# Gated cross-attention on one core: keys and values of all batches projected in the first six iterations of the second phase

## The chip, the cores and the metric

The kernel runs on one core of a Trainium2 chip. The metric is the device time of one execution in microseconds; the median of the runs is compared. TensorE (PE) multiplies matrices, VectorE (DVE), ScalarE (ACT) and GpSimd (POOL) work on tiles in SBUF, the first two also in PSUM, and SyncE (SP) issues DMAs.

## What is computed

`x` and `ctx` are 32 batches of 256 tokens with 256 features. A first layer attends from `x` to `ctx` by a symmetric divergence and adds an MLP, gated by `g_xattn`; then comes a linear layer on rounded (fp8) inputs. The second layer is what the change touches:

```python
# per batch; 16 heads of 16 features; x has gone through the first layer
xh  = layernorm(x)
q   = xh  @ w_q + b_q
k   = ctx @ w_k + b_k          # needs only the input ctx
v   = ctx @ w_v + b_v          # needs only the input ctx
att = softmax(mask(q k^T))     # 256 x 256 for each head
x   = x + gate * ((att v) @ w_o + b_o)
x   = x + gate * (silu(layernorm(x) @ fc1 + fc1_bias) @ fc2 + fc2_bias)
```

In this run nothing is masked.

## The kernel before

`phase_a` computes the first layer for all batches and leaves `X` (all 32 batches) in SBUF. `phase_b` is a software pipeline over the batches: in one iteration each engine works on eight batches at once, each at another stage. The letters are `n` (quantise, lag 0), `f` (fp8 linear, lag 1), `q` (queries, keys, values, lag 2), `m` (maxima of the scores, lag 3), `a` (exponentials and weighted values, lag 4), `o` (output projection, lag 5), `h` (MLP, first half, lag 6) and `w` (MLP, second half, and result, lag 7). With 32 batches there are 39 iterations. Those at the start and the end are written out, with the steps left out that have no batch yet or no more; the middle is a loop (`pipeline`, L51). Iteration 0 begins at 611.4 us of the profiled execution, iteration 6 at 731.6 us.

The order of the work on each engine is written out by hand, as the list of calls at the end of each engine's `iteration`. All waits are semaphore counts: `done(b)` is the count after batch `b`, `landed(b)` that of DMAs, whose semaphores alternate by parity.

Keys and values stand in it so. SyncE loads the transposed context of `f` (`load_context`, L1250). GpSimd splits it into a high and a low bf16 part (`context_parts`, L1373 and L1375). TensorE projects keys (`keys`, 12 matmuls) and, as the last step of the iteration, values (`values_in`, 12 matmuls); both are L1835. ScalarE writes the high part of the keys (L1498), VectorE the low part (`keys_low`, L1691), ScalarE copies the values to `V` (L1520), whose other 16 columns per head hold ones and give the sums of the softmax. SyncE spills keys to DRAM (`spill_keys`, L1262) and reads them back in another layout (`stack_keys`, L1279). Keys of an even and of an odd batch have one DRAM buffer each.

The score matrices of two heads at a time go twice through PSUM: `scores(i)` (L1875) for the row maxima (`maxima(i)`, VectorE, L1653), i from 0 to 7, and, one iteration later, `scores_transposed(i)` (L1892) for the exponentials (`exponential(i)`, ScalarE, L1471). Each kind has one PSUM tile, so `scores(i+1)` waits for `maxima(i)` and `scores_transposed(i+1)` for `exponential(i)`. The maxima go through two DMA transposes and two small DMAs into row 48 of `Q4` (`transpose_maxima`, `row_of_maxima`); `scores_transposed(0)` waits for them. Below, sc1 is `scores(1)` and scT7 is `scores_transposed(7)`.

Other steps on the path are: `attention_normalised` (VectorE, xh, L1742), which waits for rs2 from `inverse_std_2` on GpSimd (L1380, L1382); `mlp_normalised` (hn, L1634); `scaled` (v, L1716); `normalised_low` (xT, L1620) and `mlp_low` (hT, L1675), the low bf16 parts; `queries_low` (L1684), which waits for ScalarE's `queries_high` (L1490); `attended(t)` (L1698, L1703) and `attended_low` (L1709); `mlp_columns` (L1640); and on GpSimd `silu_parts` (L1401, L1404) and `output_bias` (L1423), which waits for xh. Four more PSUM banks are shared in turns by the other products (`TURNS`); a product waits for the last reader of the bank's previous tile.

VectorE's order before begins: hn, v, attended(0), maxima(0), xT low, attended(1), maxima(1), hT low, maxima(2), queries low, attended low, maxima(3), columns, and so on to maxima(4), keys low, attention update, maxima(5).

## Time and profile before

| | us |
|---|---|
| median of 3 runs | 1620.32 |
| lowest and highest | 1616.96, 1621.4 |
| span of the profiled execution, first to last instruction | 1614.4 |

| engine | busy us | share of the span | instructions |
|---|---|---|---|
| PE | 1486.5 | 92% | 14155 |
| DVE | 1316.4 | 82% | 3187 |
| ACT | 1135.2 | 70% | 2057 |
| POOL | 1034.7 | 64% | 1392 |

The profile shows one execution. A row of the timeline gives the start in us, the duration in us, engine, line, operation, the tile written and those read, the shape, how many instructions are merged in the row (x12), and in brackets the idle time before it with what ended it. Matmuls overlap, so that twelve of them take 1.47 us as a row and begin 1.31 us after one another as groups. A row of the windows gives the busy time of each engine in a stretch, TensorE's granted clock as a share of full speed, and the share of the DMA engines.

### The profile page before, as it was taken

What the parts mean: (1) busy time and instruction counts of PE and PEld (TensorE: products, weight loads), DVE (VectorE), ACT (ScalarE), POOL (GpSimd) and SP (SyncE); (2) the same over time, 40 slices, a digit from 0 to 9 for tenths busy, and PEclk for the clock granted to TensorE, in tenths of its full rate; (3) what the DMA queues carried; (4) which work ended last, traced back from release to release, by engine and by line L of the source; (5) the groups of instructions that cost most, each with busy time, mean ns of one, the idle gap of its engine ahead of it and who ended that gap; (6) DMA issues with size and microseconds to landing.
All of it is one profiled execution on the core that took longest, in us unless ns stands there. A gap on an engine that the chain in (4) does not pass through costs nothing.

```text
span 1614.4 us, 42641 instructions
## 1 busy us (share of the span) xinstructions
PE 1486.5 (92%) x14155; PEld 1144.6 (71%) x14155; DVE 1316.4 (82%) x3187; ACT 1135.2 (70%) x2057; POOL 1034.7 (64%) x1392
## 2 busy tenths in 40 slices
PE   4999999999999972668999999999999999999997
PEld 2788888888888861435667676777777776777666
DVE  4698888888888875778988889898988889898742
ACT  7798888888888742355666666666666666676664
POOL 4588888888888744224556565665656566565445
PEclk9999999999999995588999999999999999999999
DMA  7322222322222002332223232232223232232200
GB/s 228 96 80 66 91 72 65 96 66 69 93 65 71 2 1 92 80 119 73 80 80 87 73 85 80 85 87 81 83 78 92 72 91 74 86 85 84 64 16 22
DMA packets 197690, 125.45 MB, mean 78 GB/s; under 512 B 44400, under 2 KB 196848, under 8 KB 197360
## 3 DMA queue, kind: packets, MB, share of 16 engines
q1 hardware_dynamic: 197616, 124.48, 26.2%
q8 instruction: 44, 0.72, 0.2%
q14 instruction: 30, 0.25, 0.1%
HBM read 92.69 MB, written 25.17 MB: 73 GB/s over the span
## 4 chain that ended last, share of the span: by engine, by line
PE 48%; SPq 4%; DVE 3%; issue 2%; DMA 2%; POOL 2%; ACT 1%; POOLq 0%
PE b_bank L1835 28%; PE b_bank L1910 7%; PE b_scoreT L1892 4%; PE b_score L1875 4%; PE b_bank L1843 2%; PE b_bank L1987 1%; SPq L1306 1%; DMA b_nmT<-b_nm 1%; DMA b_yT<-b_y 1%; SPq L1290 1%; DVE b_nm L1653 1%; SPq L1279 1%; PE b_bank L1925 1%; ACT b_E L1471 1%; SPq L1315 0%
## 5 line engine op out<-in xcount | busy, mean ns | idle before, releaser
L1471 ACT ACTIVATE b_E<-b_scoreT 128x1024 f32<-128x1024 f32 x256 | 262.2, 1024 | 152.5 <-PE b_scoreT L1892 151.3
L1653 DVE TENSOR_REDUCE b_nm<-b_score 128x4 bf16<-128x1024 f32 x256 | 313.3, 1224 | 54.6 <-PE b_score L1875 48.4
L31 ACT ACT_TABLE_LOAD x157 | 201.4, 1283 | 18.6 <-PEq L1059 15.2
L1835 PE MATMUL b_bank<-f,b_YT 128*128 128x256 bf16 x1536 | 190.3, 274 | 4.7 <-POOL b_YT L1404 4.6
L890 PE MATMUL bank<-hT,W1T 128*128 128x256 bf16 x1536 | 183.3, 273 | 2.4 <-DVE hT L706 1.7
L1835 PE MATMUL b_bank<-b_hT,f 128*128 128x256 bf16 x1536 | 183.4, 273 | 0.8 <-DVE X L1749 0.8
L890 PE MATMUL bank<-W2T,G 128*128 128x256 bf16 x1024 | 171.0, 272 | 6.7 <-DVE GT L780 6.2
L1835 PEld LDWEIGHTS b_bank<-f,b_YT 128*128 128x128 bf16 x1536 | 143.5, 98 | 39.7 <-issue 19.5
L1835 PEld LDWEIGHTS b_bank<-b_hT,f 128*128 128x128 bf16 x1536 | 147.7, 98 | 30.3 <-issue 12.6
L890 PEld LDWEIGHTS bank<-hT,W1T 128*128 128x128 bf16 x1536 | 148.0, 98 | 27.7 <-ACT G L549 4.0
L1388 POOL TENSOR_TENSOR b_v<-b_v,b_e 128x512 f32<-128x512 f32 x32 | 40.6, 1269 | 195.0 <-DVE b_e L1734 195.0
L1404 POOL TENSOR_TENSOR b_YT<-b_Y,b_YT 128x512 bf16<-128x512 f32 x128 | 148.9, 1163 | 10.7
L1401 POOL TENSOR_SCALAR b_YT<-b_Y 128x512 bf16<-128x512 f32 x128 | 82.2, 642 | 104.2 <-ACT b_Y L1531 97.5
L1531 ACT ACTIVATE b_Y<-b_bank,b1f 128x256 f32<-128x256 f32 x256 | 104.2, 473 | 51.4 <-PE b_bank L1835 51.0
L890 PE MATMUL bank<-W2T,GT 128*128 128x256 bf16 x512 | 139.5, 273 | 0.0
L1910 PE MATMUL b_bank<-b_E,b_V 128*32 128x256 f32 x2048 | 134.0, 392 | 0.0
L1875 PE MATMUL b_score<-b_K,b_Q 48*128 48x256 bf16 x1024 | 102.7, 280 | 24.1 <-DVE b_nm L1653 13.1
L549 ACT ACTIVATE G<-bank,b1c 128x256 f32<-128x256 f32 x256 | 103.7, 467 | 29.4 <-PE bank L890 29.4
L890 PEld LDWEIGHTS bank<-W2T,G 128*128 128x128 bf16 x1024 | 98.3, 98 | 23.2 <-issue 12.6
L1892 PE MATMUL b_scoreT<-b_Q,b_K 49*128 49x256 bf16 x1024 | 100.7, 275 | 8.6 <-ACT b_E L1471 6.2
L1742 DVE TENSOR_SCALAR b_xh<-X,b_mv,b_rs 128x256 f32 (+1 forms) x64 | 61.9, 1006 | 43.7 <-POOL b_rs L1382 43.7
L1910 PEld LDWEIGHTS b_bank<-b_E,b_V 128*32 128x32 f32 x2048 | 57.7, 111 | 49.8 <-issue 23.4
(222 smaller groups left out, 3524.8 us busy)
## 6 DMA issues: line engine op xcount, KB each, us to landing
b_Q<-q_dram SPq DMA_DIRECT2D x192, 64.0 KB, 2.6
b_K<-k_dram SPq DMA_DIRECT2D x192, 64.0 KB, 2.8
xin<-in_x SPq DMA_DIRECT2D x32, 256.0 KB, 3.2
ctxn<-in_ctx SPq DMA_DIRECT2D x32, 256.0 KB, 2.8
mask_in<-in_mask SPq DMA_DIRECT2D x32, 256.0 KB, 3.0
X<-in_x SPq DMA_DIRECT2D x32, 256.0 KB, 4.0
ctxt<-in_ctxT SPq DMA_DIRECT2D x32, 256.0 KB, 4.2
b_ctxt<-in_ctxT SPq DMA_DIRECT2D x32, 256.0 KB, 2.8
```

The source lines that it names most:

```text
L31: act.add_instruction(mybir.InstLoadActFuncSet(name=nc.get_next_instruction_name(), act_func_set_id=which, ins=[], outs=[]))
L549: last = nc.scalar.activation(G[:, 2 * j + i], mlp_ps[j % 2][:, i], ACT.Gelu, bias=b1c[:, 2 * j + i:2 * j + i + 1])
L890: last = nc.tensor.matmul(out_tile, lhs(i, k), rhs(j, k), start=k == 0 and (i, j) == TERMS[0], stop=k == chunks[-1] and (i, j) == TERMS[-1])
L1401: nc.gpsimd.tensor_scalar(YT[:, 0, 2 * j:2 * j + 2], Y[:, 2 * j:2 * j + 2], 1.0, 0.0, ALU.mult, ALU.add).then_inc(sig["Yhi"], 1)
L1404: nc.gpsimd.tensor_tensor(YT[:, 1, 2 * j:2 * j + 2], Y[:, 2 * j:2 * j + 2], YT[:, 0, 2 * j:2 * j + 2], ALU.subtract).then_inc(sig["Ylo"], 1)
L1471: nc.scalar.activation(E[:, pair:pair + 2], scoreT_ps[:, :, :, :], ACT.Exp).then_inc(sig["E"], 1)
L1531: last = nc.scalar.activation(Y[:, 2 * j + i], bank[BANK[f"H{j}"]][:, i], ACT.Silu, bias=b1f[:, 2 * j + i:2 * j + i + 1])
L1653: nc.vector.tensor_reduce(pair, score_ps[:, :, :, :], AX.X, ALU.max, negate=True).then_inc(sig["nm"], 1)
L1835: last = nc.tensor.matmul(out_tile, lhs(i, k), rhs(j, k), start=start and k == chunks[0] and (i, j) == TERMS[0], stop=stop and k == chunks ...
L1875: last = nc.tensor.matmul(score_ps[:, odd, t], Q4[m.parity][rows, i, tile(t)], K4[m.parity][rows, i, :], start=True, stop=not mask)
L1892: last = nc.tensor.matmul(scoreT_ps[:, odd, k], K4[a.parity][rows, i, tile(k)], Q4[a.parity][rows, i, :], start=True, stop=not mask)
L1910: last = nc.tensor.matmul(bank[BANK[name]][ONE * j:ONE * (j + 1), g % 2, :], V[a.parity][:, k, i, :], E[:, i % RING, k, :], start=k == 0, ...
```

## The change

In `phase_b`, `HOISTED = (4, 5, 7, 8, 4, 4)` gives the number of batches whose keys and values are projected in iterations 0 to 5. Each such batch is a slot, and each engine's order in these iterations has eight places for slots, between its other steps. The keys go to a DRAM tensor for all batches, the values too, with their ones (512 KB a batch, float). In every iteration SyncE loads the values of batch `m` into `V` (`load_values`) and stacks the keys of batch `q` from the new tensor. The context load of the slots is issued on ScalarE's queue. Context, its split, keys and values have two buffers each; up to batch 23 the projections also have two PSUM places each (banks 6 and 8 for keys, bank 9 and half of the transposed scores' tile for values), from batch 24 on one each (6 and 9). `K` and `V` leave the turns of the banks.

The orders are written anew. On TensorE `second_product(0, 0)` moves from before `scores(1)` to behind `scores_transposed(0)`, `queries` from before `scores(2)` to behind `scores_transposed(1)`, `attended_transposed` behind `scores_transposed(2)`. On ScalarE `exponential(1)` comes before `queries_high` and `exponential(2)` before `attended_high`; table loads are left out where no step needs them. On VectorE `maxima(3)` comes before `attended_low`. On GpSimd and VectorE the rounding of iterations 0 to 2 moves to the front.

```diff
+    HOISTED = (4, 5, 7, 8, 4, 4)
+    BEFORE_ATT = sum(HOISTED[:L_ATT])
...
+        def key_bank(j):
+            return 6 if j >= BEFORE_ATT or j % 2 == 0 else 8
+
+        def value_tile(j):
+            return bank[9][:, :, :] if j >= BEFORE_ATT or j % 2 == 0 else scoreT_ps[:, 1]
...
+                def spill_keys_and_values(slot):
+                    j = hoisted(half, parity, slot)
+                    if j is None:
+                        return
+                    sp.wait_ge(sig["V"], j + 1)
+                    sp.dma_start(v_dram[j], Vs[j % 2][:, :, :, :].rearrange("p t h o -> p (t h o)")).then_inc(
+                        sig[f"vspill{j % 2}"], 16)
+                    sp.wait_ge(sig["klo"], j + 1)
+                    sp.dma_start(k_dram[j].rearrange("s (c p) n -> p (s c) n", p=P),
+                                 ks[j % 2][:, :, :, :].rearrange("p s c n -> p (s c) n")).then_inc(sig[f"kspill{j % 2}"], 16)
+
+                def load_values():
+                    sp.wait_ge(sig[f"vspill{m.parity}"], landed(m))
+                    if (due := done(m, back=2, per=NH // HG)) is not None:
+                        sp.wait_ge(sig["av_mm"], due)
+                    sp.sem_inc(sig["V_ready"], 1)
+                    sp.dma_start(V[m.parity][:, :, :, :].rearrange("p t h o -> p (t h o)"),
+                                 v_dram[bass.ds(m.number, 1)].rearrange("b p x -> p (b x)")).then_inc(sig[f"Vin{m.parity}"], 16)
...
+                def keys_high_and_values(slot):
+                    j = hoisted(half, parity, slot)
+                    if j is None:
+                        return
+                    act.wait_ge(sig["k_mm"], j + 1)
+                    if j >= 2:
+                        act.wait_ge(sig[f"kspill{j % 2}"], 16 * (j // 2))
                     for c in range(C):
...
                     last.then_inc(sig["khi"], 1)
+                    load_context(j + 2)
+                    act.wait_ge(sig["V_mm"], j + 1)
+                    act.wait_ge(sig["ones_set"], 2)
+                    if j >= 2:
+                        act.wait_ge(sig[f"vspill{j % 2}"], 16 * (j // 2))
+                    for t in range(T):
+                        last = nc.scalar.activation(Vs[j % 2][:, t, :, 0:DK],
+                                                    value_tile(j)[:, t].rearrange("p (h d) -> p h d", d=DK), ACT.Copy)
+                    last.then_inc(sig["V"], 1)
...
+                def keys_and_values(slot):
+                    j = hoisted(half, parity, slot)
+                    if j is None:
+                        return
+                    src = cT[j % 2]
+                    back = 2 if j < BEFORE_ATT else 1
+                    pe.wait_ge(sig["ctlo"], j + 1)
+                    if j >= back:
+                        pe.wait_ge(sig["klo"], j + 1 - back)
...
+                    last.then_inc(sig["k_mm"], 1)
+                    if j >= back:
+                        pe.wait_ge(sig["V"], j + 1 - back)
...
+                    last.then_inc(sig["V_mm"], 1)
...
                 if q:
                     normalised_transposed()
+                keys_and_values(0)
                 if h:
                     mlp_transposed()
-                if w:
-                    second_product(0, 0)
                 if m:
                     scores(1)
                 if a:
                     scores_transposed(0)
-                if q:
-                    queries()
+                keys_and_values(1)
+                if w:
+                    second_product(0, 0)
                 if m:
                     scores(2)
                 if a:
                     scores_transposed(1)
+                if q:
+                    queries()
+                keys_and_values(2)
+                if m:
+                    scores(3)
+                if a:
+                    scores_transposed(2)
                 if o:
                     attended_transposed()
-                if q:
-                    keys()
...
```

## Rows read from the trace of the kernel before

**Rows 1.** Windows: us, busy PE, PEld, DVE, ACT, POOL; clock, DMA share, GB/s.

```profile
611.40:678.20 66.80, 29.09 (x156) 19.64 (x156) 43.05 (x72) 18.20 (x24) 31.53 (x32) 0.58 0.34 99
678.20:731.60 53.40, 40.69 (x369) 21.79 (x369) 38.84 (x73) 28.96 (x37) 11.86 (x16) 0.80 0.37 108
850.00:1434.00 584.00, 581.80 (x6170) 418.19 (x6172) 517.04 (x1047) 394.60 (x606) 354.30 (x458) 1.00 0.29 82
```

**Rows 2.** Timeline of TensorE, one steady iteration: start us, duration us, engine, line, op.

```profile
1095.70 0.39 PE L1892 MATMUL b_scoreT<-b_Q,b_K 49*128 49x256 bf16 x4
...
1103.79 1.47 PE L1835 MATMUL b_bank<-wqkvo,b_cT 128*128 128x256 bf16 x12
...
1108.81 0.39 PE L1875 MATMUL b_score<-b_K,b_Q 48*128 48x256 bf16 x4
...
1110.77 0.39 PE L1875 MATMUL b_score<-b_K,b_Q 48*128 48x256 bf16 x4
...
1120.22 0.39 PE L1875 MATMUL b_score<-b_K,b_Q 48*128 48x256 bf16 x4
...
1123.49 0.39 PE L1892 MATMUL b_scoreT<-b_Q,b_K 49*128 49x256 bf16 x4
```

**Rows 3.** Timeline of ScalarE, then GpSimd, same iteration, after the eighth transposed score.

```profile
1097.18 1.28 ACT L31 ACT_TABLE_LOAD   x1
...
1101.84 0.71 POOL L1382 TENSOR_TENSOR b_rs<-b_ve,minus_half 128x2 f32<-128x2 f32 x1
```

**Rows 4.** Timeline of VectorE, same iteration.

```profile
1102.58 2.06 DVE L1742 TENSOR_SCALAR b_xh<-X,b_mv,b_rs 128x256 f32 x2 [1.01 <-POOL b_rs L1382]
...
1104.56 0.72 DVE L1634 TENSOR_SCALAR b_hn<-X,b_mv,b_rh 128x256 f32 x2
1105.21 1.03 DVE L1716 TENSOR_SCALAR b_v<-X,mu,rsq 128x256 f32 x2
...
1106.78 1.22 DVE L1653 TENSOR_REDUCE b_nm<-b_score 128x4 bf16<-128x1024 f32 x1
...
1109.24 1.23 DVE L1653 TENSOR_REDUCE b_nm<-b_score 128x4 bf16<-128x1024 f32 x1
...
1112.35 0.87 DVE L1684 SCALAR_TENSOR_TENSOR b_qs<-b_bank,bq_col,b_qs 128x256 bf16<-128x256 f32 x2
...
1115.01 0.22 DVE L1640 TENSOR_SCALAR b_tg<-b_rs,gate 128x2 f32<-128x2 f32 x1
...
1118.31 1.23 DVE L1653 TENSOR_REDUCE b_nm<-b_score 128x4 bf16<-128x1024 f32 x1
```

**Rows 5.** Timelines of PE, ACT, POOL, DVE near 640 us; DMA issues (KB, us to landing).

```profile
633.74 2.72 PE L1835 MATMUL b_bank<-b_xT,wqkvo 128*128 128x256 bf16 x12 [1.50 <-DVE b_xT L1620]
...
638.81 0.84 ACT L1498 ACTIVATE b_ks<-b_bank,bk_col 128x256 bf16<-128x256 f32 x2 [1.47 <-PE b_bank L1835]
...
641.70 0.66 ACT L1520 ACTIVATE b_V<-b_bank 128x256 f32<-128x256 f32 x2 [0.75 <-PE b_bank L1835]
...
645.12 0.62 POOL L1373 TENSOR_SCALAR b_cT<-b_ctxt 128x512 bf16<-128x512 f32 x1
645.82 1.15 POOL L1375 TENSOR_TENSOR b_cT<-b_ctxt,b_cT 128x512 bf16<-128x512 f32 x1
...
641.16 0.87 DVE L1691 SCALAR_TENSOR_TENSOR b_ks<-b_bank,bk_col,b_ks 128x256 bf16<-128x256 f32 x2
...
b_ctxt<-in_ctxT SPq DMA_DIRECT2D x32, 256.0 KB, 2.8
...
b_Y<-in_fc_q SPq DMA_DIRECT2D x2, 1024.0 KB, 5.2
```

**Rows 6.** Timelines of VectorE and GpSimd in iteration 7.

```profile
762.91 2.06 DVE L1742 TENSOR_SCALAR b_xh<-X,b_mv,b_rs 128x256 f32<-128x256 f32 x2 [1.96 <-POOL b_rs L1382]
...
765.84 2.05 DVE L1716 TENSOR_SCALAR b_v<-X,mu,rsq 128x256 f32<-128x256 f32 x2
...
765.11 0.67 POOL L1373 TENSOR_SCALAR b_cT<-b_ctxt 128x512 bf16<-128x512 f32 x1 [0.28 <-PE b_bank L1835]
```

More of the change, by code:

```diff
@@ L1431, in mlp_bias @@
                     add_row(w, hfb_all, "base", "zb")
+                if at_iteration(half, parity, 0):
+                    for i in range(2):
+                        nc.gpsimd.memset(Vs[i][:, :, :, :], 1.0).then_inc(sig["ones_set"], 1)
+                if n and early(half, parity):
+                    rounded()
+                context_parts(0)
                 if q:
@@ L1438, in iteration @@
                     mlp_bias()
-                if n:
+                context_parts(1)
+                context_parts(2)
+                if at_iteration(half, parity, 0):
+                    nc.gpsimd.memset(nm[:, :, :], 0.0).then_inc(sig["ones_set"], 1)
+                    for i in range(2):
+                        nc.gpsimd.memset(K4[i][:, :, :], 1.0).then_inc(sig["ones_set"], 1)
+                context_parts(3)
+                if n and not early(half, parity):
                     rounded()
@@ L1512, in heads_copy @@
                                          ACT.Copy).then_inc(sig["oS"], 1)
-                def values_copy():
-                    act.wait_ge(sig["V_mm"], done(q))
-                    act.wait_ge(sig["ones_set"], 5)
-                    if (due := done(q, back=2, per=NH // HG)) is not None:
-                        act.wait_ge(sig["av_mm"], due)
-                    for t in range(T):
-                        last = nc.scalar.activation(V[q.parity][:, t, :, 0:DK],
-                                                    bank[BANK["V"]][:, t].rearrange("p (h d) -> p h d", d=DK), ACT.Copy)
-                    last.then_inc(sig["V"], 1)
                 def silu(j):
@@ L1761, in iteration @@
                     scaled()
+                if n and early(half, parity):
+                    binades()
+                    magic()
                 if o:
@@ L1789, in iteration @@
                     base()
-                if n:
+                if n and not early(half, parity):
                     magic()
+                keys_low(3)
                 if m:
                     maxima(4)
-                if q:
-                    keys_low()
+                keys_low(4)
                 if o:
@@ L1799, in iteration @@
                     maxima(5)
+                keys_low(5)
+                if m:
                     maxima(6)
```

186 lines of the change are left out of this document (113 added, 73 removed).

## The prediction

> **What bounds the kernel now.** I read the busy shares by stage first. In the steady stretch of the second phase TensorE is busy for 581.8 of 584 us at clock 1.00, VectorE for 517.0, ScalarE for 394.6, GpSimd for 354.3 [rows 1]. So each step of 27.8 us per batch is set by TensorE's own instructions. In the first six iterations (611.4 to 731.6 us, 120.2 us) TensorE is busy for only 29.1 + 40.7 = 69.8 us, at clocks of 0.58 and 0.80 [rows 1]. There are 50.4 idle us there, and the change wants to put work into them.
>
> Then I read one steady iteration in order of time, from scores_transposed(7) (scT7, 1095.70) to the next one (1123.49): 27.79 us [rows 2]. The reader is to see which instructions of other engines already end just before TensorE comes to need them. The tightest path starts at scT7. On ScalarE its exponential is followed by the table load (1097.18) and SiLU; GpSimd splits the SiLU output and computes rs2, which ends at 1102.55 [rows 3]; only then may VectorE start xh (1102.58) [rows 4], and v, the first and the second maximum stand behind xh in VectorE's order. The first maximum starts at 1106.78 and lasts 1.22 us, so it ends at 1108.00; TensorE starts the scores that overwrite its input (sc1) at 1108.81. The second ends at 1110.47, and sc2 starts at 1110.77 [rows 2, 4]. The slack that TensorE's length hides is thus 0.8 and 0.3 us. The page's order by busy share hides this: VectorE at 88% looks free, but its order is a loop with TensorE.
>
> **What the change takes out of a steady iteration.** Keys and values are 12 matmuls each. Twelve take 1.47 us as a group and step TensorE by 1.31 us [rows 2], so 24 step it by 2.62 us. VectorE loses 0.87 us (keys low), ScalarE 0.84 + 0.66 = 1.50 us, GpSimd 1.85 us of context split [rows 5]. On SyncE's queue the 256 KB context load and the 256 KB key spill go and one 512 KB value load comes; its issue and landing end long before the next iteration's values need it, and the bytes are the same. If it had no cover, one landing between 2.8 us (256 KB) and 5.2 us (1024 KB) would stand in each iteration [rows 5].
>
> **Why those 2.62 us are not gained.** The distance from scT7 to sc2 is made of other engines' work. From scT7 to xh 1102.58 - 1095.70 = 6.88 us, from xh to the end of the second maximum 1110.47 - 1102.58 = 7.89 us [rows 2, 4]. Nothing on this path is removed or moved. With 0.06 us to TensorE it is 14.83 us, while before it was 15.07 us: 0.24 us is all that can be gained there.
>
> After sc2 the new order loses time. Before, queries stood on TensorE ahead of sc2 and queries_low on VectorE (1112.35) found its input ready. Now the second product stands before sc2, and queries come after sc2 and scT1: 0.55 us, the 12 matmuls 1.47, ScalarE 0.1 + 0.84 (the same shape as keys high), 0.06 to VectorE: 3.0 us after sc2 begins [rows 2, 6]. VectorE is done with the next maximum after only 1.8 us (0.60 for hT, 1.22) and stands still for 1.2 us. From queries_low to the columns step the rows have 1115.01 - 1112.35 = 2.66 us (queries low, attended low, the fourth maximum, in whatever order), from there to the fifth maximum 3.30 us, that maximum 1.23 [rows 4]. The scores sc5 wait for it: 3.0 + 2.66 + 3.30 + 1.23 + 0.06 = 10.25 us after sc2, where they stood 1120.22 - 1110.77 = 9.45 us after it [rows 2]. From sc5 to the next scT7 it is 3.27 us of TensorE work, as before. The loop is 14.83 + 10.25 + 3.27 = 28.35 us against 27.79: **0.56 us longer**, with 2.62 us less TensorE work in it.
>
> One more term: hn takes 0.72 us a pair while GpSimd is still, v 1.03 us with GpSimd beside its end [rows 4]. In the steady rows GpSimd idles behind the value projection while hn runs. Take away the context split, and it starts the output bias the moment xh is done, beside hn and v. The nearest rows are those of iteration 7, where GpSimd's split runs beside both: from the start of xh to the end of v 767.89 - 762.91 = 4.98 us there [rows 6], 1106.24 - 1102.58 = 3.66 us in the steady one [rows 4]. The difference, 1.32 us, lies on the loop. Bounds: 0 if the bias waits, and 1.32 from the row; the row's pattern is the new order's pattern, so I take it: 28.35 + 1.32 = 29.67 us, **1.88 us more** than 27.79.
>
> The Trainium skill, "SBUF — State Buffer", section "SBUF: two separate sides", says that VectorE and GpSimd hold their shared port pair for a whole instruction and that the loser blocks entirely. That speaks against this change. By it three of the four instructions of hn and v would each stand behind a GpSimd instruction of about 0.7 us, some 2.0 us instead of the row's 1.32; what it gives is a rival below.
>
> Twenty-six iterations (numbers 8 to 33) have this steady form: 26 x 1.88 = **+49 us**. Iterations 6 and 7 are longer anyway and I leave them as they are. The skipped table loads of the last iterations may give back 1.28 us each, twice; I leave that out.
>
> **What the change puts into the first six iterations.** 28 more batches of projections, 28 x 2.62 = 73 us of TensorE at full clock, against 50 idle us. But a slot is a chain, not only TensorE: keys 1.47, ScalarE 0.1 + 0.84, the context load of two batches on 2.8, the GpSimd split 1.85, then the keys of that batch: 7.1 us for two batches as contexts have two buffers, 3.6 us a batch [rows 5]. Each batch also moves 1 MB (256 KB in, 512 + 256 KB out); one load of 1024 KB took 5.2 us from issue to landing [rows 5]. So 3.6 to 5.2 us a slot; I take 4.0, nearer the chain, since a landing holds a fixed part that overlaps.
> - Iterations 0 to 3 hold 24 slots: 96 us. Ahead of them stand 6.6 us (value buffers' ones, the first batch's rounding and the first split on GpSimd), about 4 us for TensorE at its low clock (12 matmuls in 2.72 us instead of 1.47) [rows 2, 6], 3 us where xh holds the transposes in front of the next slot on TensorE, 3.5 us where the first scores wait for the key stack, which SyncE issues only behind the spill of the sixth slot, and 6 us for the first-layer bias behind the last slot. That is 119 us against 66.8 [rows 1]: +52.
> - Iterations 4 and 5 hold 8 slots, 6 of them new. Their 6 x 2.62 = 16 us partly fill 53.4 - 40.7 = 12.7 idle us [rows 1], but single buffers for keys and values put waits on VectorE and ScalarE between: +14.
>
> Together **+66 us**. Bounds: at 3.6 us a slot +53, with the boundaries covered too about +40, at 5.2 us a slot +104.
>
> **Sum.** The profiled execution is 1614.4 us. 1614.4 + 66 + 49 = 1729 us; the median of the runs shown, 1620.3, is 6 us above that span: **1735 us**.
>
> **Rivals.**
> 1. No wait at the shared port. The steady iteration costs 0.56 us: 15 us in all, 1701 us. For it: GpSimd's bias needs xh and may start late. Against it: the rows of iteration 7.
> 2. VectorE's chain does not bind past the first maximum, because something between (queries, attended low) comes earlier than I laid it. Then only scT7 to sc1 counts: 1108.00 + 0.06 - 1095.70 = 12.36 us where it was 13.11, a gain of 0.75 us an iteration, 20 us: 1614.4 + 66 - 20 + 6 = 1667 us. This is the most a steady iteration can gain if the rows hold.
> 3. Faster: TensorE stays the bound everywhere. It decides if a steady iteration has no wait over 0.1 us and the slots fill the idle time. Then 28 iterations gain 2.62 us, 73 us, and the start costs 73 - 50 = 23 us: 1570 us. The 581.8 busy us of 584 speak for it, the 0.8 and 0.3 us of slack against it; even with rival 2's gain the start would have to cost under 20 us.
> 4. The port blocks as the rule says: 0.68 us more in 26 iterations, 18 us: 1753 us. The skill's "SBUF — State Buffer" states it; no row here has all four instructions blocked.
> 5. The change does not do what it says: slots that cannot keep pace because spills of 768 KB a batch hold the queue that also feeds scores; over 5.2 us a slot, above 1775 us.
>
> **Chances.** Forecast 0.50, rival 1 0.20, rival 2 0.13, rival 3 0.04, rival 4 0.09, rival 5 0.04. The forecast's own range is 1705 to 1765. The range of all reaches from 1650 (rival 2 with a start of +50) to 1775. A measurement of this kernel can tell about 0.3% from no change, 5 us. Faster 0.05 (rival 3 and a corner of 2), same 0.02, slower 0.93.
>
> **What would show it.** Right: steady iterations of 29 to 30 us; TensorE busy for under 90% of them, waiting at sc1, sc2 and sc5 for a maximum (VectorE) and at hT for the attended heads; hn and v slower than before; VectorE waiting over 1 us for queries high; the first six iterations 185 us long. Wrong: a steady iteration under 27.1 us would break the chain from scT7; one of 25.2 us would mean that TensorE bounds it; no wait before queries_low would break the second step; hn and v at 0.7 us the port term; a start under 160 us the price of a slot.

## The result, and the profile after

The changed kernel takes **1786.5 us** (median of 4 runs, 1784.3 to 1788.0) against 1619.3 us for the kernel before in the same job (4 runs): ratio 1.104 (95% interval 1.102 to 1.105). The forecast was 1735 us, with a range up to 1775: the direction was right, the size was not, and the time lies 11.5 us above the range. The profiled execution has a span of 1786.2 us.

First the windows of the changed kernel by stage, with the columns of [rows 1] (us, busy PE, PEld, DVE, ACT, POOL; clock, DMA share, GB/s). The first four are iterations 0 and 1, 2, 3, and 4 and 5; the last is a steady stretch.

```profile
610.20:671.00 60.80, 31.29 (x220) 24.11 (x220) 14.98 (x35) 13.24 (x36) 26.75 (x29) 0.73 0.56 186
671.00:712.00 41.00, 24.08 (x175) 18.86 (x176) 11.60 (x30) 10.30 (x27) 19.80 (x24) 0.78 0.65 205
712.00:766.00 54.00, 39.34 (x295) 29.41 (x292) 29.40 (x50) 16.87 (x41) 23.62 (x25) 0.82 0.63 201
766.00:840.50 74.50, 57.14 (x512) 36.89 (x508) 47.04 (x87) 35.01 (x61) 24.56 (x29) 0.84 0.64 197
...
1000.00:1600.00 600.00, 537.81 (x5350) 365.16 (x5349) 486.07 (x943) 343.11 (x489) 297.92 (x390) 0.93 0.26 75
```

Two things are to be seen. The first six iterations are 230.3 us long and were 120.2 us [rows 1], with TensorE busy for 151.9 of them, so the idle time wasn't filled but grew from 50 to 78 us. And in the steady stretch TensorE, busy without a gap before, is busy for 90% of the time at a mean clock of 0.93.

To account for the whole span I took the start of VectorE's v of each iteration from both traces. Between the starts of iterations 0 and 6 there are 127.0 us before and 237.7 after: **+110.7**. Between 6 and 31 there are 701.1 and 760.3: **+59.2**. Behind that it is +3.1, ahead of it -1.2. The sum is 171.8 us, the whole difference of the spans. Over iterations 8 to 29 the mean length is 28.05 us before and 30.49 after.

Now one steady iteration of the changed kernel, TensorE: start us, duration us, engine, line, operation, number of matmuls, and in brackets the idle time and its releaser.

```profile
1202.42 0.39 PE L1980 MATMUL b_scoreT<-b_Q,b_K 49*128 49x256 bf16 x4
...
1212.09 0.60 PE L1928 MATMUL b_bank<-ident,b_xh 128*128 128x128 f32 x4
1214.67 0.66 PE L1928 MATMUL b_bank<-ident,b_hn 128*128 128x128 f32 x4 [1.98 <-DVE b_on L1778]
1215.93 0.60 PE L1960 MATMUL b_score<-b_K,b_Q 48*128 48x256 bf16 x4 [0.60 <-DVE b_nm L1725]
1216.32 0.64 PE L1980 MATMUL b_scoreT<-b_Q,b_K 49*128 49x256 bf16 x4
1216.89 2.68 PE L1920 MATMUL b_bank<-f,b_YT 128*128 128x256 bf16 x12
1219.50 0.39 PE L1960 MATMUL b_score<-b_K,b_Q 48*128 48x256 bf16 x4
...
1229.74 0.39 PE L1960 MATMUL b_score<-b_K,b_Q 48*128 48x256 bf16 x4 [0.20 <-DVE b_nm L1725]
...
1233.01 0.39 PE L1980 MATMUL b_scoreT<-b_Q,b_K 49*128 49x256 bf16 x4
```

The first and the last row are scT7, the rows at 1215.93, 1219.50 and 1229.74 are sc1, sc2 and sc5, and the twelve matmuls at 1216.89 are the second product.

The same stretch in windows shows the clock (third number from the end): at the full level, 2.4 GHz, through the idle time (first row), and near the 1.2 GHz level while the second product runs. Of the 15 second products that begin between 950 and 1400 us 12 take over 2.2 us; of 16 before, none.

```profile
1212.70:1214.60 1.90, 0.00 (x0) 0.00 (x0) 1.87 (x4) 1.85 (x2) 1.82 (x3) 1.00 0.39 131
1214.60:1216.90 2.30, 1.63 (x13) 0.82 (x14) 2.25 (x5) 0.62 (x2) 2.22 (x4) 0.80 0.41 129
1216.90:1219.50 2.60, 2.60 (x14) 1.64 (x13) 1.91 (x3) 1.02 (x1) 1.38 (x3) 0.52 0.12 25
1219.50:1222.00 2.50, 2.50 (x29) 1.72 (x28) 1.23 (x1) 1.37 (x2) 0.00 (x0) 1.00 0.18 31
```

VectorE and GpSimd in the same iteration answer to [rows 4] and [rows 6]: hn and v lie beside the output bias (GpSimd, L1466) and the SiLU split behind it (L1444). VectorE then waits for the scores that stand behind the slow product, and later for queries high.

```profile
1209.43 2.05 DVE L1817 TENSOR_SCALAR b_xh<-X,b_mv,b_rs 128x256 f32 x2 [1.71 <-POOL b_rs L1425]
1211.41 1.24 DVE L1706 TENSOR_SCALAR b_hn<-X,b_mv,b_rh 128x256 f32 x2
1212.57 1.43 DVE L1791 TENSOR_SCALAR b_v<-X,mu,rsq 128x256 f32 x2
...
1219.94 1.23 DVE L1725 TENSOR_REDUCE b_nm<-b_score 128x4 bf16<-128x1024 f32 x1 [1.12 <-PE b_score L1960]
1222.52 0.88 DVE L1756 SCALAR_TENSOR_TENSOR b_qs<-b_bank,bq_col,b_qs 128x256 bf16<-128x256 f32 x2 [1.35 <-ACT b_qs L1541]
...
1211.76 1.46 POOL L1466 TENSOR_TENSOR X<-X,gbo_all 128x256 f32 x2 [0.43 <-DVE b_xh L1817]
1213.20 0.65 POOL L1444 TENSOR_SCALAR b_YT<-b_Y 128x512 bf16<-128x512 f32 x1
```

In the start the longest bubble of TensorE, 14.86 us, is made by GpSimd's order. The rounding stands ahead of the second iteration's first context split; its second half waits for the transposes of the batch before, which SyncE issued only behind two spills and two 1024 KB loads of weights. GpSimd, then SyncE's queue, then TensorE:

```profile
647.51 1.26 POOL L1435 TENSOR_TENSOR b_y<-b_v,b_e 128x512 bf16<-128x512 f32 x1 [9.60 <-DMA b_yT<-b_y]
648.74 0.62 POOL L1416 TENSOR_SCALAR b_cT<-b_ctxt 128x512 bf16<-128x512 f32 x1
...
637.36 0.91 SPq L1259 DMA_DIRECT2D b_Y<-in_fc_q  x1
638.31 0.77 SPq L1261 DMA_DIRECT2D b_YT<-in_fc_scales  x1
639.27 5.14 SPq L1336 DMA_TRANSPOSE b_yT<-b_y  x4
...
650.64 1.68 PE L1920 MATMUL b_bank<-b_cT,wqkvo 128*128 128x256 bf16 x7 [14.86 <-POOL b_cT L1418]
```

### The profile page after: what moved, and what is told of

The parts are those of the page before. It is cut to its first block, busy times and chain, and to the rows that moved or that the text cites. A ratio compares the mean times of both kernels' runs of the same rounds, so it can differ in the third digit from the quotient of the medians.

```text
span 1786.2 us, 42891 instructions
## 1 busy us (share of the span) xinstructions
PE 1544.3 (86%) x14155; PEld 1165.3 (65%) x14155; DVE 1335.1 (75%) x3187; ACT 1116.4 (62%) x2041; POOL 1037.1 (58%) x1392
## 3 DMA queue, kind: packets, MB, share of 16 engines
q1 hardware_dynamic: 198128, 149.65, 27.6%
## 4 chain that ended last, share of the span: by engine, by line
PE 28%; DVE 12%; issue 7%; POOL 5%; ACT 4%; DMA 4%; SPq 4%; DVEq 1%; POOLq 0%; ACTq 0%
PE b_bank L1920 18%; DVE b_nm L1725 4%; PE b_scoreT L1980 3%; PE b_score L1960 3%; PE b_bank L2002 2%; DVE b_v L1791 2%; ACT L31 2%; DVE b_hn L1706 2%; DMA b_ctxt<-in_ctxT 1%; POOL b_YT L1447 1%; ACT b_Y L1592 1%; POOL b_YT L1444 1%; DMA b_nmT<-b_nm 1%; SPq L1307 1%; DVE b_xh L1817 1%
## 5 line engine op out<-in xcount | busy, mean ns | idle before, releaser
L1522 ACT ACTIVATE b_E<-b_scoreT 128x1024 f32<-128x1024 f32 x256 | 262.2, 1024 | 235.5 <-PE b_scoreT L1980 235.2
L1920 PE MATMUL b_bank<-f,b_YT 128*128 128x256 bf16 x1536 | 212.4, 294 | 4.6 <-POOL b_YT L1447 4.6
L1920 PEld LDWEIGHTS b_bank<-f,b_YT 128*128 128x128 bf16 x1536 | 153.1, 105 | 51.7 <-issue 22.2
L1444 POOL TENSOR_SCALAR b_YT<-b_Y 128x512 bf16<-128x512 f32 x128 | 82.8, 646 | 109.6 <-ACT b_Y L1592 103.0
L1960 PE MATMUL b_score<-b_K,b_Q 48*128 48x256 bf16 x1024 | 107.5, 291 | 32.8 <-DVE b_nm L1725 25.6
L1920 PE MATMUL b_bank<-b_cT,wqkvo 128*128 128x256 bf16 x384 | 61.8, 325 | 64.0 <-POOL b_cT L1418 60.9
L1980 PE MATMUL b_scoreT<-b_Q,b_K 49*128 49x256 bf16 x1024 | 106.8, 289 | 9.6 <-ACT b_E L1522 5.5
L1766 DVE SCALAR_TENSOR_TENSOR b_ks<-b_bank,bk_col,b_ks 128x256 bf16<-128x256 f32 x64 | 28.0, 479 | 111.9 <-ACT b_ks L1559 111.9
```

What stands on the lines that cost most here:

```text
L1444: nc.gpsimd.tensor_scalar(YT[:, 0, 2 * j:2 * j + 2], Y[:, 2 * j:2 * j + 2], 1.0, 0.0, ALU.mult, ALU.add).then_inc(sig["Yhi"], 1)
L1522: nc.scalar.activation(E[:, pair:pair + 2], scoreT_ps[:, :, :, :], ACT.Exp).then_inc(sig["E"], 1)
L1920: last = nc.tensor.matmul(out_tile, lhs(i, k), rhs(j, k), start=start and k == chunks[0] and (i, j) == TERMS[0], stop=stop and k == chunks ...
L1960: last = nc.tensor.matmul(score_ps[:, odd, t], Q4[m.parity][rows, i, tile(t)], K4[m.parity][rows, i, :], start=True, stop=not mask)
L1980: last = nc.tensor.matmul(scoreT_ps[:, odd, k], K4[a.parity][rows, i, tile(k)], Q4[a.parity][rows, i, :], start=True, stop=not mask)
```

## The experiments

The table puts all fifteen together. "Period" is the mean from v to v over iterations 8 to 29, "first six" the distance of v from iteration 0 to 6, "clock" TensorE's mean granted clock from 950 to 1400 us (not taken where left blank), "slow" the second products of over 2.2 us among those that begin there. Periods, distances and clocks are those of the one profiled execution of each kernel; the time is the median, the ratio is to the kernel before in the same job.

| kernel | us | ratio, 95% interval | period | first six | clock | slow |
|---|---|---|---|---|---|---|
| before | 1617 to 1620 | 1 | 28.05 | 127.0 | 1.00 | 0 of 16 |
| changed | 1786.5 | 1.102 to 1.105 | 30.49 | 237.7 | 0.94 | 12 of 15 |
| e1 old orders | 1745.1 | 1.073 to 1.083 | 29.11 | 235.8 | 0.97 | 7 of 15 |
| e2 second product back | 1794.8 | 1.106 to 1.114 | 30.73 | 237.3 | 0.95 | 14 of 14 |
| e3 bias waits | 1746.0 | 1.074 to 1.084 | 28.86 | 236.4 | 0.97 | 7 of 15 |
| e4 before, short products | 1682.9 | 1.037 to 1.047 | 30.63 | | 0.94 | 15 of 15 |
| e5 matmuls behind the idle | 1795.6 | 1.105 to 1.116 | 30.39 | 237.5 | 0.98 | 0 of 15 |
| e6 late rounding | 1773.7 | 1.088 to 1.102 | 30.40 | 226.5 | |  |
| e7 e1 and e3 | 1708.7 | 1.051 to 1.063 | 27.46 | 235.7 | 1.00 | 0 of 17 |
| e8 third context buffer | 1781.8 | 1.097 to 1.104 | 30.42 | 233.6 | |  |
| e9 e4 with waits | 1594.3 | 0.980 to 0.991 | 27.45 | | 1.00 | 0 of 17 |
| e10 before, GpSimd's order | 1607.5 | 0.991 to 0.996 | 27.85 | 121.0 | 1.00 |  |
| e11 matmuls in the idle | 1760.4 | 1.086 to 1.092 | 29.17 | 236.2 | 1.00 | 0 of 15 |
| e12 e7, e6 and e8 | 1690.7 | 1.043 to 1.049 | 27.41 | 220.9 | 1.00 |  |
| e13 split one slot ahead | 1770.7 | 1.090 to 1.101 | 30.17 | 216.7 | |  |
| e14 short slot products | 1756.5 | 1.082 to 1.089 | 30.30 | 204.7 | |  |
| e15 slots 8, 8, 8, 8, 0, 0 | 1795.9 | 1.105 to 1.112 | 30.64 | 244.9 | |  |

### The steady iteration: order, shared port and clock

**e1** undoes the reordering and keeps everything else.

```diff
 PE:  + second_product(0, 0) ahead of scores(1);  queries ahead of scores(2)
      + attended_transposed ahead of keys_and_values(2);  scores_transposed(2) ahead of scores(3)
 ACT: + queries_high ahead of exponential(1);  attended_high ahead of exponential(2)
 DVE: + attended_low ahead of maxima(3)
```

> The changed kernel (1786 us) with the old relative orders of the second product, queries, attended heads (TensorE), queries high and attended high (ScalarE) and attended low (VectorE); only the keys and values stay in the first six iterations. Chain theory (a steady iteration is a loop from scores_transposed(7) over ScalarE, GpSimd and VectorE back to TensorE, and the new order puts 1.2 us of waiting for queries into it): a steady iteration of 28.2 us instead of 30.5, 26 times, about 1726 us; if TensorE still falls to its low clock after the wait for the attended heads, up to 1.3 us an iteration more, 1760 us. Rival, the order is harmless and the loss is in the first six iterations alone: 1780 us or more. Rival, TensorE's own work bounds a steady iteration once the order is the old one: 25.2 us, 1650 us.

Measured 1745.1 us. VectorE's wait for queries high, 23.9 us between 950 and 1400 us in the changed kernel, is gone from the list of waits. TensorE still idles ahead of the transposes of hn (27.6 us in 15 iterations). Undoing the order gives 1.38 us an iteration. Part of it may come through the clock, since only 7 of 15 second products are slow now; the six moves were not tried one by one, e2 apart.

**e2** moves one piece back.

```diff
+                if w:
+                    second_product(0, 0)
                 if m:
                     scores(1)
```

> The changed kernel with one step moved back: the first part of the second product stands before scores(1) again, where it fills TensorE's wait for the second maximum. Chain theory: scores(2) waits for the second maximum either way; what goes is the low clock of the second product if the next step takes no harm from it: 29.4 us a steady iteration, 1758 us. If the low clock hits whatever follows the wait for the attended heads, scores(1) comes 2.6 us after it and the time stays within 5 us of 1786. Rival, the order is harmless: 1786 us.

Measured 1794.8 us, 8 us more than the changed kernel. The low clock only meets other instructions: the transposes of hn take 1.11 us and the product 2.51 us, now in every iteration, and the first scores stand behind both. Moving the second product back alone gains nothing while the clock falls.

**e3** makes GpSimd's output bias wait.

```diff
 def output_bias():
+    if n and not early(half, parity):
+        pool.wait_ge(sig["v"], done(n))
```

> The changed kernel with one more wait: GpSimd starts the output bias only when v is written, so no GpSimd instruction runs beside hn and v. Port theory: hn and v take 1.4 us together instead of 2.6, the loop is 0.9 to 1.2 us shorter in each of 26 iterations, 1755 to 1762 us, and if TensorE's idle time before hT becomes too short for its clock to fall, another 0.9 us an iteration, down to 1735 us. Rival, the two engines do not hinder each other on the path that counts: 1786 us, or slower by GpSimd's later start.

Measured 1746.0 us. hn and v run at 0.72 and 0.73 us, TensorE's idle ahead of the transposes is 0.66 us in the mean instead of 1.85, and 7 of 15 second products are slow. VectorE of e3:

```profile
1225.39 0.72 DVE L1708 TENSOR_SCALAR b_hn<-X,b_mv,b_rh 128x256 f32 x2
1226.03 0.73 DVE L1793 TENSOR_SCALAR b_v<-X,mu,rsq 128x256 f32 x2
```

One wait on an engine that is busy for half of the steady stretch gives 1.63 us an iteration. Port and clock both have a part in it; this run doesn't divide them.

**e7** is both.

> The changed kernel with the old relative orders of the second product, queries and attended heads (as e1) and with GpSimd's output bias behind VectorE's v (as e3). Theory (two different losses: the order costs VectorE's wait of 1.35 us for the queries, the bias costs the shared time at hn and v and with it the clock): the steady iteration is 27.0 to 27.4 us, 1722 us (1710 to 1732). Rival (both edits only cure the same fall of the clock, each already whole): 1738 to 1748. If the gains are additive without overlap: 1705.

Measured 1708.7 us. 1.38 and 1.63 are 3.01 us, the period falls by 3.03: the gains add whole, and the rival that each alone already cures all of the clock's part is out (7 slow products stay with each, none with both). It came nearer to the "no overlap" figure than to my theory. What is left, 27.46 us, is 0.6 us below the kernel before although TensorE has 2.62 us less to do, and e9 stops at the same 27.45 us. The forecast's own terms with the old order give 14.83 + 9.45 + 3.27 = 27.55 us. But in e7 the two maxima end 0.8 and 0.3 us before TensorE needs them, as before; where TensorE waits is for the attended heads (0.65 us an iteration) and, with the key matmuls gone, for an exponential of ScalarE (12.8 us in 16 times). So the period comes near the length that the forecast read off, but the waits that set it are others.

**e5** and **e11** test the clock alone: 14 or 16 matmuls whose output is overwritten, placed behind the idle (e5) and inside it (e11).

```diff
 e5, in mlp_transposed, behind free("hT"):
+    for i in range(14):
+        nc.tensor.matmul(bank[BANK["hT"]][:, i % 2], wqkvo[:, 0, 0, 0, tile(0)], wf[:, 0, :], start=True, stop=True)
 e11, ahead of mlp_transposed, from iteration 8 on:
+    free("F2")
+    for i in range(16): the same, into bank[BANK["F2"]]
```

> The changed kernel with one addition: ahead of its wait for the normalised MLP input (hT), TensorE issues 14 matmuls of 256 columns whose result is overwritten (each some 0.12 us, together 1.6 us), inside the 1.98 us in which it stood idle in the steady iteration 1202 to 1233 of the changed kernel. Nothing is waited for less. Theory (the loss over 28 us an iteration is the granted clock, which falls to half of full after this idle and makes the second product 2.68 instead of 1.47 us long): the second product is 1.5 us again, the maxima come 1.0 to 1.2 us earlier, 26 iterations give 29 us, less up to 5 us in iterations where the new matmuls don't fit the idle: 1762 us (1752 to 1770). Rival (the idle itself is the loss, the clock costs nothing on the path, or falls from another cause): 1784 to 1800.

> The changed kernel with 16 matmuls of 256 columns (each some 0.11 us) into the second product's free bank ahead of the transposition of hn, so inside TensorE's idle of 1.98 us. In e5 they stood behind the wait for the bank of hT, which VectorE's attended heads free, and so came after the idle: they cost 1.70 us and the second product was 1.49 us at full clock, together no gain. Theory (half clock costs 1.2 us on the path): now they cost nothing, the second product is 1.5 us, the iteration 29.3 to 29.6 us, 1760 us (1752 to 1768). Rival (the clock falls in any case, or sc1 and sc2 aren't what VectorE waits for last): 1780 to 1795.

e5: 1795.6 us. TensorE waits for the bank of hT, which the attended heads free, and the matmuls came behind that wait. At full clock they cost 1.70 us and saved 1.2 where the product had been slow. And the clock still fell in 6 of 15 iterations (mean 0.98): there the added matmuls met the low clock and took 2.9 to 3.2 us, and the product behind them didn't. Cost and saving nearly cancel in the period. One iteration of each kind:

```profile
1211.24 1.70 PE L2024 MATMUL b_bank<-wf,wqkvo 128*128 128x256 bf16 x14 [1.99 <-DVE b_on L1778]
1212.78 0.60 PE L1928 MATMUL b_bank<-ident,b_hn 128*128 128x128 f32 x4
...
1213.86 1.49 PE L1920 MATMUL b_bank<-f,b_YT 128*128 128x256 bf16 x12
...
1148.77 2.96 PE L2024 MATMUL b_bank<-wf,wqkvo 128*128 128x256 bf16 x14 [1.99 <-DVE b_on L1778]
...
1153.06 1.49 PE L1920 MATMUL b_bank<-f,b_YT 128*128 128x256 bf16 x12
```

e11: 1760.4 us (1748.9 to 1764.3), 1760 expected. TensorE of e11:

```profile
1223.51 1.91 PE L2117 MATMUL b_bank<-wf,wqkvo 128*128 128x256 bf16 x16
1225.51 0.66 PE L1928 MATMUL b_bank<-ident,b_hn 128*128 128x128 f32 x4
1226.65 0.39 PE L1960 MATMUL b_score<-b_K,b_Q 48*128 48x256 bf16 x4 [0.48 <-DVE b_nm L1725]
...
1227.20 1.48 PE L1920 MATMUL b_bank<-f,b_YT 128*128 128x256 bf16 x12
```

Useless work in an idle stretch makes the kernel 26 us faster: the half clock is on the path. Nothing else was changed, so this is shown, not argued. Over 26 iterations that is 1.0 us each, and 12 slow products in 15, at 2.68 - 1.47 = 1.21 us, give the same 1.0. The profiled execution of e11 was its fastest run (1748.9 us); its period is 1.32 us shorter, which is the upper end.

**e4** and **e9** do the reverse: the kernel before, with TensorE relieved of key and value matmuls (4 of the 24 of both together stay).

```diff
 e4, before.py, from iteration 6 on, in column_projection("K") and row_projection("V"):
-    last = product(..., range(C))
+    last = nc.tensor.matmul(..., start=True, stop=True)
 e9, besides, on GpSimd:
+    output_bias: pool.wait_ge(sig["v"], done(n))
     output_bias()
+    context_parts()          # for batch q; before: last in the iteration ahead, for batch f
 and on SyncE: transpose_rounded() ahead of load_context()
```

> The kernel before with most of the work of the projections left out from iteration 6 on: 4 matmuls instead of 24 for keys and values (so keys and values of those batches are not the reference's), all waits, copies and DMAs kept, nothing moved. It takes 2.2 us of TensorE work out of each of 28 iterations at no price. Chain theory: the steady iteration gains only its slack, about 0.6 us, 17 us in all: 1603 us. Rival, TensorE bounds it (581.8 of 584 us busy): 2.2 us each, 61 us: 1559 us.

> The kernel before with the key and value products cut to 4 of 24 matmuls each from iteration 6 on (its output is then not the reference's, as e4), and with GpSimd's output bias and context split put behind VectorE's v: the split moves from the end of an iteration to behind the output bias of the next. Theory (e4 lost 65 us because GpSimd, no longer held back by the value product, ran beside hn and v, which took 1.94 and 1.54 us, and because TensorE's clock fell in the wait that followed): hn and v are 0.7 us each, no half clock at the second product, steady iteration 27.0 to 27.5 us, 1600 us (1588 to 1612). Rival (less TensorE work lowers the clock by itself or the chain is longer for a reason not seen): 1640 or more.

e4: 1682.9 us, 65 us slower with less to do; both sides of my expectation were below the kernel before. Its rows, VectorE, GpSimd, TensorE:

```profile
1100.57 2.06 DVE L1742 TENSOR_SCALAR b_xh<-X,b_mv,b_rs 128x256 f32 x2 [1.71 <-POOL b_rs L1382]
1102.56 1.94 DVE L1634 TENSOR_SCALAR b_hn<-X,b_mv,b_rh 128x256 f32 x2
1104.42 1.54 DVE L1716 TENSOR_SCALAR b_v<-X,mu,rsq 128x256 f32 x2
...
1102.44 0.67 POOL L1373 TENSOR_SCALAR b_cT<-b_ctxt 128x512 bf16<-128x512 f32 x1
1103.19 1.16 POOL L1375 TENSOR_TENSOR b_cT<-b_ctxt,b_cT 128x512 bf16<-128x512 f32 x1
1104.31 1.50 POOL L1423 TENSOR_TENSOR X<-X,gbo_all 128x256 f32 x2
...
1106.64 1.12 PE L1843 MATMUL b_bank<-ident,b_hn 128*128 128x128 f32 x4 [2.64 <-DVE b_on L1703]
1107.55 2.59 PE L1835 MATMUL b_bank<-f,b_YT 128*128 128x256 bf16 x12
```

In the kernel before the value product held GpSimd back from its context split until hn was over (1105.28):

```profile
1105.45 0.64 POOL L1373 TENSOR_SCALAR b_cT<-b_ctxt 128x512 bf16<-128x512 f32 x1 [0.96 <-PE b_bank L1835]
```

With the product short, GpSimd runs beside hn and v, TensorE waits 2.64 us, and its clock falls. e9 gives the waits back by hand: hn 0.72, v 0.72, clock 1.00, 1594.3 us. Between e4 and e9 TensorE's work is the same; the difference is GpSimd's order and waits (and SyncE's swap, whose part was not tried alone), and it is 89 us. How it divides between port and clock isn't shown.

### The first six iterations

**e6** puts the rounding back to its late place, **e8** gives the contexts a third buffer.

```diff
 e6: early():
-    return isinstance(half, int) and 2 * half + parity < L_MAX
+    return False
 e8: ctxt, load_context, context_parts:
-    two("ctxt", ...);  load_context(j + 2);  ctxt[j % 2]
+    three buffers;     load_context(j + 3);  ctxt[j % 3]
```

> The changed kernel with the rounding of the quantised update at its later place on GpSimd (behind the fourth context) and on VectorE in every iteration, as from the seventh on; nothing else. Theory (in the second and third iteration the contexts stand behind the rounding, which waits for the transposes of the batch before it, queued on SyncE behind spills and 1 MB loads; TensorE stands 14.9 and 7.3 us): both waits go, up to 3 us come back where the rounding is now late, 1767 us (1762 to 1775). Rival (the landing of the contexts under 200 GB/s of other transfers is what each slot waits for; the rounding hides in it): 1780 to 1790. Second rival (the rounding placed later delays the quantised product of the next iteration and costs as much): over 1790.

> The changed kernel with three instead of two buffers for the contexts, each loaded three slots ahead instead of two; the split, the products and the spills stay. Theory (with two buffers a slot's load is issued only behind the copy of the keys two slots back, and load 3.2 to 6.0 us, split 1.8 us, products and copy then follow each other; GpSimd waits 52.8 us for contexts before 840 us, and TensorE 60.9 us for the split): the wait for contexts falls below 20 us and the first six iterations give back 25 to 35 us, 1757 us (1748 to 1765). Rival (a load that comes earlier only moves the wait to the next late thing, the spill of keys that the copy waits for, 11.7 us, or the rounding on GpSimd): 1774 to 1790.

e6: 1773.7 us, 13 us less than the changed kernel where 19 were expected; 11 of them lie in the first six. e8: 1781.8 us, 5 us less, hardly clear of noise: the wait that I had blamed was cured and the time stayed. GpSimd's waits before 850 us in the changed kernel, where one line held 52.8 us, and then in e8 (total us, times, longest):

```profile
POOL b_cT L1416 <- DMA b_ctxt<-in_ctxT: 52.8, 14, 12.6
```

```profile
POOL b_ve L1423 <- DVE b_mv L1679: 33.8, 5, 9.2
POOL b_v L1431 <- DVE b_e L1810: 32.9, 6, 8.9
POOL b_cT L1416 <- PE b_bank L1921: 21.5, 7, 4.8
...
POOL b_cT L1416 <- DMA b_ctxt<-in_ctxT: 8.5, 3, 6.1
```

This is a moved wait: 44 us of waiting for landings are gone, and most of it is back as waits for TensorE (30.2 us with the next line of that list, 3.5 in the changed kernel) and for VectorE (66.7 us in the first two rows, 54.4 in the changed kernel).

**e13** lets GpSimd split each context one slot ahead, into a third buffer; **e14** cuts the slots' products; **e15** lays the slots out otherwise.

```diff
 e13: cT in three buffers; context_parts(slot) splits context j + 1 (the first call 0 and 1)
 e14: keys_and_values(slot):
-    last = product(...)      # 24 matmuls a slot
+    last = nc.tensor.matmul(...)   # 4 a slot
 e15:
-    HOISTED = (4, 5, 7, 8, 4, 4)
+    HOISTED = (8, 8, 8, 8, 0, 0)
```

> The changed kernel with three buffers for the split contexts, and GpSimd splitting each context one slot ahead of its place in the order; two context buffers as before. Since the third context buffer of e8 took the wait for landings from 52.8 to 8.5 us and gave 5 us only, GpSimd's order is the next suspect: a split stands behind the rounding and the deviations, which wait for VectorE (26 and 28 us). Theory (that order alone holds the products): TensorE's 60.9 us of waiting for splits before 840 us falls to 30, 1758 us (1748 to 1768). Rival (the slots and each iteration's own chain run one after the other on every engine, so the wait moves to the next engine): 1775 to 1790.

> The changed kernel with the key and value products of each slot cut from 24 matmuls together to 4 (the output is then not the reference's); loads, splits, copies and spills stay. TensorE loses some 3.0 to 3.7 us of work in each of 32 slots. Theory (a slot is a chain of load, split, product, copy with two in flight, 8 us for two; the key product's 1.5 to 1.9 us is the one part of it that goes): 0.7 us a slot, 1763 us (1750 to 1772). Rival (TensorE sets the start): 80 us less, 1700 to 1720. Second rival (as in e4: less work on TensorE, lower clock, more shared time): 1786 or more.

> The changed kernel with its 32 slots laid out as 8 in each of the first four iterations and none in the next two, instead of 4, 5, 7, 8, 4, 4. The forecast took the longer of an iteration's own chain and its slots; the trace of the changed kernel looks as if both add up: 66.8 us of the first four iterations before and 24 slots of 4.0 us are 163 us, measured 156. Theory (they add up): the same 32 slots cost the same wherever they stand, 1786 us (1774 to 1798). Rival (the longer of the two counts): four iterations of 32 to 35 us and two of 26.7 us, 185 to 195 us instead of 230: 1741 to 1752.

e13: 1770.7 us, between theory and rival; the first six are 21 us shorter, so GpSimd's order is at most half of the miss of 44 us there (the profile is that of its fastest run, 1760.1 us, against a median of 1770.7; by the medians the whole gain is 16 us). e14: 1756.5 us: with 20 of a slot's 24 matmuls gone the first six are 33 us shorter. Had TensorE set the start, 80 us would have gone (the rival of the expectation); its wait for splits rises to 74.4 us instead. e15 decides between adding and taking the longer. The lengths of the iterations, from v to v:

| iteration | 0 | 1 | 2 | 3 | 4 | 5 |
|---|---|---|---|---|---|---|
| before | 4.4 | 15.0 | 20.0 | 27.5 | 21.1 | 38.9 |
| changed (4, 5, 7, 8, 4, 4 slots) | 24.7 | 37.7 | 46.1 | 49.1 | 32.0 | 48.2 |
| e15 (8, 8, 8, 8, 0, 0) | 39.4 | 50.8 | 51.3 | 46.1 | 20.9 | 36.4 |

Without slots, iterations 4 and 5 fall back to what they were before. With slots, each pays on top of its own length: (237.7 - 127.0) / 32 = 3.5 us a slot in the one layout, (244.9 - 127.0) / 32 = 3.7 in the other. Had the longer of two parts counted, e15 would have taken 35 to 45 us less; it took 9 us more. Over the first four iterations alone a slot costs 3.8 us in both layouts (157.6 and 187.6 us against 66.9), but not evenly: 5.1 us in iteration 0 of the changed kernel, 2.3 in iteration 3 of e15 and in iteration 5 of the changed kernel. So an iteration with a long chain of its own does take in a part of its slots' time, far less than all of it.

### Versions made of what helped

**e12** is e7 with e6 and e8.

> The changed kernel with all that helped so far: old relative orders and output bias behind v (e7, 1708.7 us), the late rounding (e6, 13 us less than the changed kernel) and three context buffers (e8). Theory (the start and the steady iterations lose for separate reasons and the gains add): 1668 us (1655 to 1685). Rival (late rounding and the third buffer cure the same wait): 1685 to 1700. In no case below the kernel before: its 26 later iterations would have to be 24 us long, which VectorE's chain of 27 us forbids.

Measured 1690.7 us, 4.6% over the kernel before. The late rounding and the third buffer give 15 us in the first six (11 and 4 alone): they add, but each is smaller than I had put in, and the 1668 us that I expected were missed by 23. The time lies in the rival's range, but its reason, one wait cured twice, isn't what the first six show. **e10** takes what was learnt to the kernel before, with no projections moved.

```diff
 before.py, GpSimd:
+    output_bias: pool.wait_ge(sig["v"], done(n))
+    output_bias(); context_parts()        # context split here, for batch q
+    inverse_std_2() ahead of silu_parts(h, 0)
 SyncE: transpose_rounded() ahead of load_context()
```

> The kernel before with GpSimd's order alone changed: output bias behind VectorE's v, the context split behind that bias in the next iteration, and the inverse deviation of the second normalisation ahead of the SiLU split of the first piece (in the trace of before GpSimd began that split 0.2 us ahead of the statistics, and VectorE then waited 1.01 us for the deviation). All of the computation is done. Theory (VectorE's chain sets the iteration of the kernel before too): xh starts up to 1.0 us earlier, v is 0.73 instead of 1.03 us, 26 iterations of 0.5 to 0.9 us, 1600 us (1588 to 1608). Rival (TensorE, busy 93% there, sets the iteration): 1611 to 1622. Slower rival (GpSimd's later split holds TensorE's keys): over 1622.

Measured 1607.5 us, ratio 0.994 (0.991 to 0.996): the only version with all of the computation that is faster than the kernel before, by 10 us. The gain is 6 us in the first six and 0.20 us an iteration, not 0.5 to 0.9. TensorE is busy for all 450.0 us of the window 950 to 1400, so an earlier xh has nothing to shorten, and as GpSimd's SiLU splits now lie beside hn, hn takes longer:

```profile
1120.67 1.91 DVE L1745 TENSOR_SCALAR b_xh<-X,b_mv,b_rs 128x256 f32 x2
1122.50 1.94 DVE L1637 TENSOR_SCALAR b_hn<-X,b_mv,b_rh 128x256 f32 x2
1124.36 0.72 DVE L1719 TENSOR_SCALAR b_v<-X,mu,rsq 128x256 f32 x2
```

## Why the prediction was right and where it failed

The profiled span grew by 171.8 us where the forecast had 66 + 49 = 115. Of the 57 us between them 44 lie in the start and 13 in the rest. The 6 us that the forecast added for the median above the span came to 0.3 us, which by luck hid 6 us of the miss. Two steps failed: TensorE's clock behind its new wait was put at nothing, and the slots were taken to replace the first iterations' own length.

**Right: the saving isn't gained.** Most of the chain that the forecast laid from scT7 held. From sc2 to sc5 10.25 us were forecast and 10.24 measured, from sc5 to scT7 3.27 and 3.27, from scT7 to xh 6.88 and 7.01; VectorE waited 1.35 us for queries high where 1.2 were forecast; TensorE waits at sc1, sc5 and hT as forecast, but not at sc2, where its own second product ended last. e1 prices the new order at 1.38 us an iteration, where the forecast's chain has 10.25 - 9.45 = 0.80. Five slow products fewer in 15 iterations, at 1.21 us each, may be 0.4 of the difference (an estimate); the rest isn't settled. Rivals 2 and 3, where TensorE's length or a shorter chain would have counted, needed 27.1 or 25.2 us and are out at 30.49; even e7, with the orders and the bias cured, is at 27.46.

**Half right: the shared port.** From the start of xh to the end of v it is 4.57 us in the changed kernel against 3.66 before: 0.91 us, between the bounds 0 and 1.32. The row of iteration 7 was the wrong pattern: there a context split lay beside hn and v, here the output bias, which begins 0.35 us behind hn, and the start of a SiLU split. e4 has split and bias and shows 5.39 us, 1.73 more than before, which is above my row. The Trainium skill, "SBUF — State Buffer", section "SBUF: two separate sides", has the loser block for the whole instruction; by it I had 2.0 us (rival 4). The trace agrees with the rule in this: one by one, three of the four instructions of hn and v take 0.92, 0.81 and 0.70 us, where each takes 0.40 us in e3, and each of the three ends 0.15 us behind the end of a GpSimd instruction (0.74, 0.78 and 0.65 us) that ran beside it. So rival 4 had the pattern, three held instructions, and the price too high: they lose 1.23 us together, not 2.0, and the kernel before already lost 0.30 of that at the end of v. Against the 3.35 us of e3, where GpSimd is held back, the changed kernel loses 1.22 us and e4 2.04.

**Missed: TensorE's clock.** This step was not in the sum at all. The chain from scT7 to sc2 took 17.08 us, 0.93 more than forecast: +0.13 at xh, -0.41 at the port, and +1.21 at the second product, 2.68 us instead of 1.47. I had named the wait at hT among the signs and gave it no price. But behind this wait the clock falls, and with it comes the next loss. I had a row for this: in the start of the kernel before, 12 matmuls take 2.72 us [rows 5], and I used it only for the start. e11 gives the price on the path, 1.0 us an iteration by the medians and up to 1.32 by its profile. The steady part was forecast at +49 us and came to +62 with the end.

**Missed: the slots stand on top.** The price of a slot was about right: 4.0 us forecast, 3.5 to 3.7 measured over the 32 slots (110.7 / 28 = 4.0 for each batch that wasn't there before). Wrong was the sentence that 24 slots and 23 us of edges replace the first four iterations' own 66.8 us. They add to it: 66.8 + 24 x 3.7 = 156 us; the windows show 155.8, the forecast had 119. The miss is 37 us there and 7 us in iterations 4 and 5 (74.5 us, forecast 67). Idle time of TensorE was taken for room. But every engine works its slots and its own chain off in one fixed order, so that a slot waits while that chain waits; e13, e14 and e15 fit this reading, and only e13 tries it directly, for one engine. GpSimd's order alone is worth 21 us at most (e13), the early rounding 11 us (e6), late landings 4 us (e8); with 20 of a slot's 24 matmuls gone 78 us remain (e14). How the rest divides among ScalarE's and VectorE's orders wasn't tried.

## What to carry to other kernels

Ask what holds an engine back today before taking its releaser away: here a matmul group that seemed to be mere cost kept GpSimd off VectorE and kept TensorE's clock up, and without it a lighter kernel was 65 us slower until GpSimd got an explicit wait. Idle time in a pipeline's fill is not room by itself: here work put into the orders of all five engines came largely on top. And an idle gap ahead of a long matmul group can have two prices, the wait and the slower group behind it: look at the granted clock behind each gap.

## What the runs showed of the hardware

TensorE's clock fell from 1.00 to 0.80 and 0.52 in the windows behind an idle stretch of 1.98 us, and rose again behind the slow product. The length of that stretch alone doesn't decide: behind 1.85 us in the mean the clock fell in 12 of 15 iterations of the changed kernel, behind 1.84 us in 7 of 15 of e1, behind 0.66 us still in 7 of 15 of e3. e7 and e9, with gaps of 0.65 and 0.56 us, show no fall; what tells e3 from e7 is open. Matmuls placed behind the gap (e5) didn't keep the clock up: it fell in 6 of 15 iterations, and they ran at it themselves. Matmuls placed inside the gap (e11) left the clock at 1.00 in all 15.

A VectorE instruction (128x256, f32, 0.40 us alone) beside a GpSimd instruction took 0.70 to 1.32 us in the iterations read of the changed kernel and of e4 (xh, hn and v), and in each of these cases it ended 0.15 us behind the GpSimd instruction. With the two kept apart by a wait (e3, e9) it took 0.40 us.
